# A spectral filter and MLP on one core: mirrored rows folded ahead of the transform along h, and that transform moved between the two mixings

## The chip, the cores and the metric

The kernel runs on one core of a Trainium2 chip. The metric is the device time of one execution in microseconds (us). The engines named here are TensorE (PE in the profile), VectorE (DVE), ScalarE (ACT), GpSimd (POOL) and SyncE (SP, which only issues DMAs).

## The reference

Two layers run over two images of 128 x 128 positions with 128 channels, in fp32. `afno_filter` mixes channels in the frequency domain, in blocks of 16 channels:

```python
def afno_filter(x, w1, b1, w2, b2):
    xf = jnp.fft.rfft2(x, axes=(1, 2), norm='ortho')
    ...
    o1r = jax.nn.relu(xr @ w1[0] - xi @ w1[1] + b1[0])   # einsum per block of channels
    o1i = jax.nn.relu(xi @ w1[0] + xr @ w1[1] + b1[1])
    o2r = o1r @ w2[0] - o1i @ w2[1] + b2[0]
    o2i = o1i @ w2[0] + o1r @ w2[1] + b2[1]
    ...                                                  # softshrink, 0.01
    return jnp.fft.irfft2(yf, s=(H, W), axes=(1, 2), norm='ortho') + x
...
    h = afno_filter(layer_norm(x, n1_g, n1_b), w1, b1, w2, b2) + x
    residual = h
    h = jax.nn.gelu(layer_norm(h, n2_g, n2_b) @ mw1 + mb1, approximate=False)
    return h @ mw2 + mb2 + residual
```

## The kernel before

The program makes four steps, one for each layer and image (`s` = 0 to 3). Each step has four stages on TensorE, one behind the other:

- `dft_w`: the transform along w, 128 matmuls of 128 x 128 x 128 (line 581), four into one PSUM bank. In step 0 ScalarE copies each bank to the arena in SBUF; in steps 1 to 3 ScalarE and VectorE take turns (line 362).
- `filter_`: 34 units, in 17 pairs (q = 0 and 1, one for each half of the channels). A unit goes through six operations on three engines: the transform along h (`dft_h`, line 591, four matmuls into bank q), a copy to `gsb` by ScalarE (`g_copy`, line 871), the first mixing (`mix1`, line 611, 64 x 64 tiles, bank 2 + q), bias and relu to `osb` by ScalarE (`o_relu`, line 878), the second mixing (`mix2`, line 649, 64 x 64 tiles, banks 4 to 7), and bias and softshrink by VectorE (`shrink`, lines 1119, 1121, 1134). Pair 1 has a single frequency only, and pairs 0 and 1 together need `edges` (line 688).
- `idft_h` (line 724), the inverse transform along h, whose banks ScalarE and VectorE copy out (line 389).
- `mlp`: the inverse transform along w (lines 743 and 749), layer norm, and the two products of the MLP with the gelu between them.

Nothing schedules this at run time: each engine runs its own instructions in the order of the program text, and counters (semaphores) hold one engine until another has come far enough. In the filter the order on TensorE is, for each p, mix1 of pair p + 1, mix2 of pair p, dft_h of pair p + 3. On ScalarE it is the two copies of pair p + 2, then the two relus of pair p + 1 (`batch`, line 959 and on).

What holds whom around the change:

- `gsb` and `osb` each have one buffer for each q. So `g_copy` of unit n waits until the first mixing of unit n - 2 has read `gsb` (`act.wait_ge(m1_mm, UNITS * s + n - 1)`), and `o_relu` of unit n until the second mixing of unit n - 2 has read `osb` (`act.wait_ge(m2_mm, UNITS * s + n - 1)`).
- `dft_h` of a unit writes bank q, and waits until the copy of the unit before it with the same q is done (`pe.wait_ge(g_out, ...)`).
- `mix1` of pair p + 1 waits for its two copies and for the relus of pair p, which read banks 2 and 3.
- `mix2` waits for its relu and for VectorE's first operation on the bank that it writes (`v_out`).

Of the kernel before, what the change touches and what calls it, by code (L numbers as in the profile page):

```python
# [75 lines left out]
CONSTS = 7 * P + MASKS  # L76
EVEN = KWS + 1
PB = 8
# [14 lines left out]
HELD_BANK = (6, 7, 0, 2)  # L93
# [9 lines left out]
def dft_constants():  # L103
# [10 lines left out]
    fh = np.concatenate([np.cos(turn * np.outer(h, k)), np.sin(turn * np.outer(h, k[1:-1]))], 1) * scale  # L114
    k_of = np.concatenate([k, -k[1:-1]])
    ih = np.concatenate([np.cos(turn * np.outer(k_of, h[:HALF + 1])),
                         np.sin(turn * np.outer(k_of, -h[HALF + 1:]))], 1) * scale

# [7 lines left out]
    parts = [fw.reshape(P, P), fh, ih, de.reshape(P, P).T, do.reshape(P, P).T, np.eye(P), reverse]  # L126
# [27 lines left out]
def afno(nc, x, consts, params, out):  # L154
    ctx = ExitStack()
    with ctx:
# [27 lines left out]
        paired = [a.rearrange("p (t h e) -> p t h e", h=H, e=2) for a in flat]  # L184
        spectra = [a.rearrange("p (k a g b d) -> p k a g b d", a=2, g=2, b=2, d=QUART) for a in flat]
        columns_of = [a.rearrange("p (q c k) -> p q c k", q=2, c=HALF) for a in flat]

        def rows_of(s):

            return paired[s % 2]  # L190

        def spec_of(s):

            return spectra[(s + 1) % 2]

# [14 lines left out]
        mask = cst[:, 7 * P:].rearrange("p (s b) -> p s b", s=4)  # L210
# [328 lines left out]
        def _(pe):  # L539
# [45 lines left out]
            def dft_h(s, n):  # L585
# [10 lines left out]
            def mix1(s, p):  # L596
# [39 lines left out]
            def mix2(s, p):  # L636
                kws = 1 if p == 1 else GROUP
                if s == 0 and p == 1:
                    pe.wait_ge(r_dve, R_DVE)
                if p >= 2:  # L640
                    pe.wait_ge(v_out, UNITS * s + 2 * p - 2)
                for q in range(2):
                    pe.wait_ge(o_out, UNITS * s + 2 * p + q + 1)
                    for i in range(kws):
                        at_ = GROUP * HALF * q + HALF * i
# [931 lines left out]
```

## Time and profile before

| | us |
|---|---|
| median of 3 runs | 1629.3 (1629.04 to 1630.48) |
| the profiled execution, its own time | 1629.48 |
| its span in the trace | 1627.7 |
| TensorE busy | 1556.1 (96%) |
| VectorE busy | 990.3 (61%) |
| ScalarE busy | 889.3 (55%) |
| GpSimd busy | 620.4 (38%) |

The span is the part of the execution that the trace covers; 1.8 us lie around it. An engine that is busy for most of the span is likely what bounds the kernel, but what one stage costs is read from the timeline of that stage: which engine works without a gap there, and what ends the gaps of the others.

### The profile page before, as it was taken

The page shows a single profiled execution, that of the slowest core. Times are in us where ns is not written, and L with a number is a line of the kernel's source. Part 1 is how long each engine was busy: PE and PEld are TensorE (multiplying, and loading weights), DVE is VectorE, ACT ScalarE, POOL GpSimd, SP SyncE. Part 2 cuts the span into 40 slices and gives each one's busy share as a digit, 9 for nine tenths or more (in the row PEclk, how much of TensorE's full clock was granted, in tenths as well). Part 3 has the DMA queues.
Part 4 walks back from the last instruction along what each step waited for, and adds up shares of the span by engine and source line. Part 5 has one row for each costly group of instructions (what it writes and reads, how often), then busy time and mean ns, then how long its engine had stood idle before and what let it go on. Part 6 is the DMA issues. An engine that isn't in the chain of part 4 may idle for free.

```text
span 1627.7 us, 43919 instructions
## 1 busy us (share of the span) xinstructions
PE 1556.1 (96%) x16132; PEld 1379.1 (85%) x16132; DVE 990.3 (61%) x2433; ACT 889.3 (55%) x1638; POOL 620.4 (38%) x782
## 2 busy tenths in 40 slices
PE   0999999999999899999999989999999989999999
PEld 0987888888998788888898888888889879888888
DVE  7967556656537665665655766565663675555553
ACT  5544366666534356666643436666662443666665
POOL 5800046776800017677660003667673000111111
PEclk9999999999999999999999999999999999999999
DMA  8410713333300062333420052333331006011111
GB/s 225 172 45 3 241 49 107 104 99 119 98 15 3 9 240 86 108 101 99 124 79 2 3 203 66 104 110 97 104 111 46 3 3 207 27 39 32 32 39 46
DMA packets 168583, 138.30 MB, mean 85 GB/s; under 512 B 10882, under 2 KB 132484, under 8 KB 168452
## 3 DMA queue, kind: packets, MB, share of 16 engines
q1 hardware_dynamic: 167268, 136.24, 26.6%
q8 instruction: 96, 1.57, 0.4%
q10 hardware_dynamic: 1184, 0.20, 0.1%
q14 instruction: 35, 0.29, 0.1%
HBM read 69.30 MB, written 67.11 MB: 84 GB/s over the span
## 4 chain that ended last, share of the span: by engine, by line
PE 93%; DVE 3%; ACT 1%; SPq 1%; DMA 1%; issue 1%; POOL 0%; ACTq 0%; DVEq 0%
PE ps L797 27%; PE ps L591 8%; PE ps L611 8%; PE ps L581 7%; PE ps L763 7%; PE ps L765 7%; PE ps L724 7%; PE ps L764 7%; PE ps L757 3%; PE ps L649 3%; PE ps L743 3%; PE ps L749 3%; SPq L431 1%; DMA first<-in_x_dram 1%; PE ps L779 1%
## 5 line engine op out<-in xcount | busy, mean ns | idle before, releaser
L797 PEld LDWEIGHTS ps<-mw,gel 128*128 128x128 f32 x4000 | 520.6, 191 | 42.3
L797 PE MATMUL ps<-mw,gel 128*128 128x128 f32 x4000 | 523.7, 274 | 0.0
L907 ACT ACTIVATE gel<-ps,mb1f 128x512 f32<-128x512 f32 x500 | 343.7, 687 | 250.6 <-PE ps L765 219.7
L1473 POOL TENSOR_TENSOR arena<-arena,mb2rep 128x512 f32<-128x512 f32 x125 | 160.2, 1282 | 634.5 <-ACT hn L893 634.5
L763 PE MATMUL ps<-hth,mw1h 128*128 128x512 f32 x512 | 259.7, 507 | 4.5 <-DVE vsb L1119 1.7
L1462 POOL TENSOR_SCALAR arena<-xnext,rstd,shift 128x128 f32<-128x128 f32 x360 | 159.4, 462 | 207.6 <-DVE shift L1356 207.6
L893 ACT ACTIVATE hn<-arena,shift,rstd 128x128 f32 (+1 forms) x512 | 221.6, 483 | 16.8 <-DVE shift L1356 16.8
L765 PE MATMUL ps<-hth,mw1l 128*128 128x512 f32 x512 | 202.1, 395 | 0.0
L764 PE MATMUL ps<-htl,mw1h 128*128 128x512 f32 x512 | 200.8, 392 | 0.0
L1203 DVE TENSOR_TENSOR arena<-ps,arena 128x512 f32 (+1 forms) x60 | 41.5, 691 | 252.0 <-PE ps L749 233.4
L871 ACT COPY gsb<-ps 128x512 f32<-128x512 f32 x128 | 69.1, 589 | 159.1 <-PE ps L611 153.0
L1220 DVE TENSOR_TENSOR htl<-ps,hth 128x512 fp32r<-128x512 f32 x128 | 88.2, 689 | 97.5 <-ACT hth L901 97.5
L1119 DVE TENSOR_TENSOR vsb<-ps,b2cols 128x512 f32<-128x512 f32 (+1 forms) x136 | 90.3, 664 | 88.2 <-PE ps L649 88.2
L611 PE MATMUL ps<-gsb,w1s 64*64 64x252 f32 (+5 forms) x2304 | 128.0, 359 | 9.2 <-ACT osb L878 6.2
L591 PE MATMUL ps<-cst,arena 128*128 128x128 f32 x1024 | 131.3, 281 | 2.3 <-ACT gsb L871 2.0
L1420 POOL TENSOR_TENSOR gz<-arena,gain 128x512 f32<-128x512 f32 x96 | 123.8, 1290 | 7.0
L591 PEld LDWEIGHTS ps<-cst,arena 128*128 128x128 f32 x1024 | 119.8, 191 | 6.9 <-ACT gsb L871 2.5
L581 PE MATMUL ps<-cst,arena 128*128 128x128 f32 x1024 | 121.4, 282 | 0.9 <-POOL arena L1433 0.9
L581 PEld LDWEIGHTS ps<-cst,arena 128*128 128x128 f32 x1024 | 120.9, 196 | 1.0 <-DVE arena L1085 1.0
L724 PEld LDWEIGHTS ps<-cst,arena 128*128 128x128 f32 x1024 | 115.3, 192 | 7.2 <-DVE arena L1134 6.2
L724 PE MATMUL ps<-cst,arena 128*128 128x128 f32 x1024 | 116.0, 275 | 4.7 <-DVE arena L1134 4.7
L901 ACT CAST hth<-ps 128x512 fp32r<-128x512 f32 x128 | 75.2, 587 | 80.1 <-PE ps L757 80.1
(111 smaller groups left out, 2125.6 us busy)
## 6 DMA issues: line engine op xcount, KB each, us to landing
arena<-aside SPq DMA_DIRECT2D x128, 256.0 KB, 4.8
aside<-gz SPq DMA_DIRECT2D x96, 256.0 KB, 3.0
between<-xout SPq DMA_DIRECT2D x62, 256.0 KB, 2.3
out_dram<-xout SPq DMA_DIRECT2D x62, 256.0 KB, 2.3
xnext<-between SPq DMA_DIRECT2D x60, 256.0 KB, 3.0
aside<-first SPq DMA_DIRECT2D x32, 256.0 KB, 2.3
xnext<-in_x_dram SPq DMA_DIRECT2D x30, 256.0 KB, 3.1
first<-in_x_dram SPq DMA_DIRECT2D x1, 960.0 KB, 7.4
```

Of the source, the lines that this page charges most:

```text
L581: mm = pe.matmul(ps[:, 2 + cg % 4, P * i:P * i + P], rows_of(s)[:, (GROUP * cg + i) // 2, :, i % 2], FW, start=True, stop=True)
L591: mm = pe.matmul(ps[:, q, P * i:P * i + P], spec_of(s)[:, GROUP * b + i, q].rearrange("p g r c -> p (g r c)"), FH, start=True, stop=True)
L611: mm = pe.matmul(to[:, :, dst[0]:dst[1]], w1s[own_rows, kind, q].rearrange("p r c -> p (r c)"), gsb[own_rows, q, j0:j1, src[0]:src[1]], st ...
L724: mm = pe.matmul(ps[:, cg % 4, P * i:P * i + P], y_of(s)[:, q, ch, :], IH, start=True, stop=True)
L763: pe.matmul(bank, h, hth[:, r % 2, :], start=True, stop=False)
L764: pe.matmul(bank, h, htl[:, r % 2, :], start=False, stop=False)
L765: pe.matmul(bank, l, hth[:, r % 2, :], start=False, stop=True).then_inc(f1_mm, 1)
L797: mm = pe.matmul(ps[:, r % 2, P * i:P * i + P], gel[:, r % 2, m, P * i:P * i + P], mw2[:, s // IMAGES, m, :], start=(m == 0 and i == 0), s ...
L893: ins = act.activation(hn[:, r % 2, i, :], row, ACT.Identity, bias=shift[:, r // 2, r % 2 * ROWS + i:r % 2 * ROWS + i + 1], scale=rstd[:, ...
L907: act.activation(gel[:, r % 2, m, :], ps[:, 2 + m % 2], ACT.Gelu, bias=mb1f[:, s // IMAGES, m:m + 1]).then_inc(gelu_out, 1)
L1462: ins = pool.tensor_scalar(zrow(s + 1, h0 + k), pairs(xnext[:, r, k, :]), rstd[:, r // 2, row:row + 1], shift[:, r // 2, row:row + 1], ALU ...
L1473: pool.tensor_tensor(t, t, b, ALU.add).then_inc(mb2_done, 1)
```

## The change

It has four parts. Those on steps 1 to 3 leave step 0 as it was.

1. **Folding (steps 1 to 3).** The rows of an image are laid in SBUF so that slot i and slot i + 64 hold rows that mirror each other. The transform along w is made in tiles of 128 rows by 64 columns: two channel groups, g = 0 and 1, go to the two halves of the PSUM partitions, the upper 64 slots to one bank and the lower 64 to the next (`mirrored`). ScalarE copies the upper bank to `hn`; VectorE writes the sum and the difference of both to the arena (`fold_out`, two operations for two banks).
2. **Transform along h in 64 x 64 tiles (steps 1 to 3).** The sums give the cosine part (65 columns), the differences the sine part (95 columns with the mirrored half). Both units of a pair go in one call, so that the four tiles of the array (two halves of the rows, two of the columns) are addressed one after another. The call waits for both copies. Step 0 keeps the 128 x 128 form, one unit behind the other.
3. **PSUM banks by unit.** The second mixing of q = 0 writes banks 4 and 5, that of q = 1 banks 6 and 7, each with a wait and a count of its own; before, a pair wrote 4 and 5 or 6 and 7 by turns and counted once. Two banks of the MLP's held tile move from 6 and 7 to 2 and 3.
4. **Order.** The transform along h of pair p + 3 is issued ahead of the second mixing of pair p, not behind it, in all four steps.

The inverse transform's columns, the rows that the last transform reads, and the VectorE operations behind it are turned round to the new order of rows; their number and size stay.

```diff
-HELD_BANK = (6, 7, 0, 2)
+HELD_BANK = (2, 3, 0, 2)
...
+        folded = [a.rearrange("p (k o a b d) -> p k o a b d", o=2, a=2, b=2, d=QUART) for a in flat]
...
             def evicted(s, cg):
                 if s == 0:
                     pe.wait_ge(a_act, cg + 1)
-                elif cg % 2:
-                    pe.wait_ge(a_dve, CGROUPS // 2 * (s - 1) + cg // 2 + 1)
-                else:
-                    pe.wait_ge(a_act, CGROUPS + CGROUPS // 2 * (s - 1) + cg // 2 + 1)
+                else:
+                    pe.wait_ge(a_dve, CGROUPS * (s - 1) + cg + 1)
...
                 for cg in range(CGROUPS):
-                    if s and cg == 3:
-                        pe.wait_ge(lo_out, TILES * s)
+                    if s:
+                        mirrored(s, cg // 2, cg % 2)
+                        continue
...
+            def mirrored(s, d, sign):
+
+                if d == 1 and sign:
+                    pe.wait_ge(lo_out, TILES * s)
+                if d >= 2 and not sign:
+                    evicted(s, 2 * d - 3)
+                q, slots = d // 8, slice(HALF, H) if sign else slice(0, HALF)
+                for i in range(GROUP):
+                    for g in range(2):
+                        t = KWS // 2 * q + KWS // 4 * g + GROUP // 2 * (d % 8) + i // 2
+                        mm = pe.matmul(ps[HALF * g:HALF * g + HALF, 2 + 2 * (d % 2) + sign, P * i:P * i + P],
+                                       rows_of(s)[:, t, slots, i % 2], FW, start=(i == 0), stop=True,
+                                       skip_group_check=True)
+                mm.then_inc(s1_mm, 1)
+
+            def dft_h(s, n, units=(0,)):
+                if s:
+                    g = spectrum_of(n + units[-1])
+                    if g >= 2:
+                        pe.wait_ge(g_out, 2 * BATCHES * s + g - 1)
+                    for i in range(GROUP):
+                        for o in range(2):
+                            for u in units:
+                                q = (n + u) % 2
+                                for x in range(2):
+                                    own_rows = slice(HALF * x, HALF * x + HALF)
+                                    cols = slice(HALF * (x ^ q), HALF * (x ^ q) + HALF)
+                                    dst = slice(P * i, P * i + EVEN) if o == 0 else slice(P * (i + 1) - FOLD_O, P * (i + 1))
+                                    mm = pe.matmul(ps[cols, q, dst],
+                                                   folded_of(s)[own_rows, GROUP * (g // 2) + i, o, q].rearrange(
+                                                       "p r c -> p (r c)"),
+                                                   FOLDS[o][own_rows], start=(i == 0 and o == 0), stop=True,
+                                                   skip_group_check=True)
+                    mm.then_inc(s2_mm, len(units))
+                    return
+                for u in units:
+                    whole_dft_h(s, n + u)
...
             def mix2(s, p):
                 kws = 1 if p == 1 else GROUP
-                if s == 0 and p == 1:
-                    pe.wait_ge(r_dve, R_DVE)
-                if p >= 2:
-                    pe.wait_ge(v_out, UNITS * s + 2 * p - 2)
                 for q in range(2):
+                    if p:
+                        pe.wait_ge(v_out, UNITS * s + 2 * p + q - 1)
+                    elif s == 0 and q:
+                        pe.wait_ge(r_dve, R_DVE)
+                    if p == EDGE_PAIR and q:
+                        pe.wait_ge(y_done, (UNITS + 1) * s + 2 * EDGE_PAIR + 1)
                     pe.wait_ge(o_out, UNITS * s + 2 * p + q + 1)
...
-                mm.then_inc(m2_mm, 2)
+                    mm.then_inc(m2_mm, 1)
...
                 for p in range(PAIRED):
                     if p + 1 < PAIRED:
                         mix1(s, p + 1)
-                    if p == EDGE_PAIR + 1:
-                        pe.wait_ge(y_done, (UNITS + 1) * s + 2 * EDGE_PAIR + 2)
-                    mix2(s, p)
+                    if p + 3 < PAIRED:
+                        dft_h(s, 2 * p + 6, (0, 1))
                     if p == EDGE_PAIR:
                         edges(s)
-                    if p + 3 < PAIRED:
-                        for q in range(2):
-                            dft_h(s, 2 * p + 6 + q)
+                    mix2(s, p)
...
                     if cg >= 4:
                         turned(s, cg - 4)
+                    elif s and cg >= 2:
+                        pe.wait_ge(gelu_out, CHUNKS * (TILES * s - 1) + cg - 1)
...
+            def upper_copy(s, q, j, r):
+
+                act.wait_ge(s1_mm, CGROUPS * s + CGROUPS // 2 * q + 4 * j + 2 * r + 1)
+                act.copy(hn[:, r].rearrange("p a b -> p (a b)"), ps[:, 2 + 2 * r]).then_inc(a_act, 1)
...
+            def fold_out(s, q, j, r):
+
+                dve.wait_ge(a_act, CGROUPS + CGROUPS // 2 * (s - 1) + CGROUPS // 4 * q + 2 * j + r + 1)
+                dve.wait_ge(s1_mm, CGROUPS * s + CGROUPS // 2 * q + 4 * j + 2 * r + 2)
+                upper = hn[:, r].rearrange("p a b -> p (a b)").rearrange("p (i k r) -> p k r i", i=GROUP, r=2)
+                lower_ = ps[:, 3 + 2 * r].rearrange("p (i k r) -> p k r i", i=GROUP, r=2)
+                for o, op in enumerate((ALU.add, ALU.subtract)):
+                    dst = folded_of(s)[:, :, o, q, :, bass.ds(GROUP * (2 * j + r), GROUP)]
+                    dve.tensor_tensor(dst, upper, lower_, op).then_inc(a_dve, 1)
...
-                at_ = GROUP * HALF * q
-                src = ps[:, 4 + 2 * odd:6 + 2 * odd, at_:at_ + HALF * kws].rearrange(
+                src = ps[:, 4 + 2 * q:6 + 2 * q, 0:HALF * kws].rearrange(
```

TensorE, step 0, in the middle of the filter. `gsb,w1s` is the first mixing, `w2s,osb` the second, `cst,arena` the transform along h. Before:

```order
22 L649 MATMUL ps<-w2s,osb 64x64 x32
23 L591 MATMUL ps<-cst,arena_51 128x128 x8
24 L611 MATMUL ps<-gsb,w1s 64x4x65 x4
25 L611 MATMUL ps<-gsb,w1s 64x4x63 x12
26 L649 MATMUL ps<-w2s,osb 64x64 x32
27 L591 MATMUL ps<-cst,arena_51 128x128 x8
28 L611 MATMUL ps<-gsb,w1s 64x4x65 x4
29 L611 MATMUL ps<-gsb,w1s 64x4x63 x12
30 L649 MATMUL ps<-w2s,osb 64x64 x32
```

The change at the same place:

```order
22 L649 MATMUL ps<-cst,arena_51 128x128 x8
23 L709 MATMUL ps<-w2s,osb 64x64 x32
24 L669 MATMUL ps<-gsb,w1s 64x4x65 x4
25 L669 MATMUL ps<-gsb,w1s 64x4x63 x12
26 L649 MATMUL ps<-cst,arena_51 128x128 x8
27 L709 MATMUL ps<-w2s,osb 64x64 x32
28 L669 MATMUL ps<-gsb,w1s 64x4x65 x4
29 L669 MATMUL ps<-gsb,w1s 64x4x63 x12
30 L649 MATMUL ps<-cst,arena_51 128x128 x8
```

The transform (x8, both units of a pair) stood behind the second mixing (x32), and stands ahead of it. (The lines are those of each program: `dft_h` is line 591 before and 649 behind the change, `mix1` 611 and 669, `mix2` 649 and 709.)

TensorE, step 1, a turn of the filter, before:

```order
334 L611 MATMUL ps<-gsb,w1s 64x4x65 x4
335 L611 MATMUL ps<-gsb,w1s 64x4x63 x12
336 L649 MATMUL ps<-w2s,osb 64x64 x32
337 L591 MATMUL ps<-cst,arena_50 128x128 x8
338 L611 MATMUL ps<-gsb,w1s 64x4x65 x4
339 L611 MATMUL ps<-gsb,w1s 64x4x63 x12
340 L649 MATMUL ps<-w2s,osb 64x64 x32
```

The change at the same place, one pair:

```order
366 L669 MATMUL ps<-gsb,w1s 64x4x65 x4
367 L669 MATMUL ps<-gsb,w1s 64x4x63 x12
368 L633 MATMUL ps<-cst,arena_50 64x65 x4
369 L633 MATMUL ps<-cst,arena_50 64x95 x4
370 L633 MATMUL ps<-cst,arena_50 64x65 x4
371 L633 MATMUL ps<-cst,arena_50 64x95 x4
372 L633 MATMUL ps<-cst,arena_50 64x65 x4
373 L633 MATMUL ps<-cst,arena_50 64x95 x4
374 L633 MATMUL ps<-cst,arena_50 64x65 x4
375 L633 MATMUL ps<-cst,arena_50 64x95 x4
376 L709 MATMUL ps<-w2s,osb 64x64 x32
377 L669 MATMUL ps<-gsb,w1s 64x4x65 x4
```

Eight matmuls of 128 x 128, which stood behind the second mixing, have become 32 of 64 x 64 with 65 and 95 columns, and stand between the two mixings.

VectorE, step 1, the first banks of the transform along w, before (with the semaphores waited for):

```order
537 L362 ISA [waits s1_mm]
538 L362 COPY arena_50<-ps 128x64x2x4
539 L1091 REGISTER_ALU
540 L362 ISA [waits s1_mm]
541 L362 COPY arena_50<-ps 128x64x2x4
```

The change:

```order
537 L1162 ISA [waits a_act]
538 L1167 ISA [waits s1_mm]
539 L1167 TENSOR_TENSOR arena_50<-hn,ps 128x64x2x4
540 L1167 ISA
541 L1167 TENSOR_TENSOR arena_50<-hn,ps 128x64x2x4
```

A copy of every second bank has become a sum and a difference for every two banks, which wait for ScalarE (`a_act`) and TensorE (`s1_mm`).

## Rows read from the trace of the kernel before

**Rows 1.** The page: engines' busy us; the chain that ended last, by engine

```profile
PE 1556.1 (96%) x16132; PEld 1379.1 (85%) x16132; DVE 990.3 (61%) x2433; ACT 889.3 (55%) x1638; POOL 620.4 (38%) x782
...
PE 93%; DVE 3%; ACT 1%; SPq 1%; DMA 1%; issue 1%; POOL 0%; ACTq 0%; DVEq 0%
```

**Rows 2.** Filter, steps 0, 3: length, busy PE, PEld, DVE, ACT, POOL, clock

```profile
76.53:163.55 87.02, 81.80 (x1898) 70.49 (x1896) 63.66 (x116) 37.39 (x67) 1.16 (x1) 1.00 0.11 37
...
1255.49:1342.54 87.05, 81.40 (x1889) 69.67 (x1887) 58.73 (x108) 38.19 (x68) 0.00 (x0) 1.00 0.01 3
```

**Rows 3.** Timeline, PE, step 1's filter: start, duration, line, out<-in, count

```profile
505.88 1.94 PE L611 MATMUL ps<-gsb,w1s 64*64 64x260 f32 x32
507.64 1.11 PE L649 MATMUL ps<-w2s,osb 64*64 64x64 f32 x64
508.68 2.05 PE L591 MATMUL ps<-cst,arena 128*128 128x128 f32 x16
510.66 1.94 PE L611 MATMUL ps<-gsb,w1s 64*64 64x260 f32 x32
512.42 1.11 PE L649 MATMUL ps<-w2s,osb 64*64 64x64 f32 x64
```

**Rows 4.** Timeline of ScalarE and VectorE in the same turn

```profile
507.88 1.07 ACT L871 COPY gsb<-ps 128x512 f32<-128x512 f32 x2 [2.52 <-PE ps L611]
...
508.82 0.69 DVE L1119 TENSOR_TENSOR vsb<-ps,b2cols 128x512 f32<-128x512 f32 x1 [0.89 <-PE ps L649]
508.88 1.27 ACT L878 ACTIVATE osb<-ps,vectors 128x512 f32<-128x512 f32 x2
```

**Rows 5.** Timeline of step 1's filter, behind the short second mixing

```profile
483.00 0.41 PE L649 MATMUL ps<-w2s,osb 64*64 64x64 f32 x16
483.25 1.07 ACT L871 COPY gsb<-ps 128x512 f32<-128x512 f32 x2 [3.17 <-PE ps L611]
...
483.88 2.05 PE L591 MATMUL ps<-cst,arena 128*128 128x128 f32 x16 [0.47 <-ACT gsb L871]
```

**Rows 6.** Timeline of the last two pairs of step 1's filter

```profile
550.32 1.14 PE L649 MATMUL ps<-w2s,osb 64*64 64x64 f32 x64
551.53 0.69 DVE L1119 TENSOR_TENSOR vsb<-ps,b2cols 128x512 f32<-128x512 f32 x1 [0.53 <-PE ps L649]
551.59 1.27 ACT L878 ACTIVATE osb<-ps,vectors 128x512 f32<-128x512 f32 x2 [3.15 <-PE ps L649]
...
552.42 1.18 PE L649 MATMUL ps<-w2s,osb 64*64 64x64 f32 x64 [0.96 <-ACT osb L878]
```

**Rows 7.** The transform along w, step 1: stretch, then VectorE's copies

```profile
439.82:469.97 30.15, 30.15 (x258) 30.15 (x257) 11.06 (x16) 9.38 (x16) 9.07 (x8) 1.00 0.16 53
...
L362 DVE COPY arena<-ps x48: 691/692/693, 442.0 to 1255.8; 128x512 f32 x48
...
466.53 0.69 DVE L362 COPY arena<-ps 128x512 f32 x1 [1.19 <-PE ps L581]
```

**Rows 8.** Timeline of VectorE ahead of it: a sum of PSUM and SBUF

```profile
435.06 0.69 DVE L1234 TENSOR_TENSOR xout<-ps,arena 128x512 f32<-128x512 f32 x1
435.67 2.15 DVE L1365 TENSOR_SCALAR arena<-xlast,rstd,shift 128x128 f32<-128x128 f32 x8
```

**Rows 9.** Timeline of the start of step 1's filter

```profile
469.97 2.30 PE L591 MATMUL ps<-cst,arena 128*128 128x128 f32 x16
...
472.31 0.59 ACT L871 COPY gsb<-ps 128x512 f32<-128x512 f32 x1 [0.58 <-PE ps L591]
...
473.04 2.14 PE L611 MATMUL ps<-gsb,w1s 64*64 64x195 f32 x64 [0.77 <-ACT gsb L871]
```

**Rows 10.** Two stretches at the end of step 1's filter

```profile
545.00:549.00 4.00, 2.46 (x96) 2.01 (x92) 2.78 (x5) 2.26 (x4) 0.00 (x0) 1.00 0.00 0
553.00:557.00 4.00, 2.23 (x47) 1.51 (x38) 3.86 (x8) 1.38 (x2) 0.00 (x0) 1.00 0.01 4
```

**Rows 11.** Timeline of VectorE in step 2: weights scaled between copies

```profile
849.78 0.72 DVE L1022 TENSOR_SCALAR w1s<-w1s,swapped 128x64 f32<-128x64 f32 x4
```

More of the change, by code:

```diff
@@ L75 @@
 MASKS = 4 * BLOCKS
-CONSTS = 7 * P + MASKS
 EVEN = KWS + 1
+FOLD_E, FOLD_O = EVEN, P - EVEN + KWS // 2
+MASK_AT = 7 * P + FOLD_E + FOLD_O
+CONSTS = MASK_AT + MASKS
 PB = 8
@@ L113, in dft_constants @@
     fw[:, 0, 1] = cos[:, KWS]
-    fh = np.concatenate([np.cos(turn * np.outer(h, k)), np.sin(turn * np.outer(h, k[1:-1]))], 1) * scale
-    k_of = np.concatenate([k, -k[1:-1]])
+    ks = np.concatenate([[0, KWS], np.arange(2, KWS, 2), np.arange(1, KWS, 2)])
+    fh = np.concatenate([np.cos(turn * np.outer(h, ks)), np.sin(turn * np.outer(h, ks[2:]))], 1) * scale
+    k_of = np.concatenate([ks, -ks[2:]])
+    fold_e, fold_o = fh[:HALF, :EVEN].copy(), fh[:HALF, P - FOLD_O:].copy()
+    fold_e[-1] = scale * (ks % 2 == 0)
+    fold_o[:, :KWS // 2] = 0
+    fold_o[-1] = -scale * (np.arange(FOLD_O) < KWS // 2)
+    folds = np.tile(np.concatenate([fold_e, fold_o], 1), (2, 1))
     ih = np.concatenate([np.cos(turn * np.outer(k_of, h[:HALF + 1])),
                          np.sin(turn * np.outer(k_of, -h[HALF + 1:]))], 1) * scale
+    ih[:, HALF:] = ih[:, :HALF - 1:-1].copy()
     de = 2 * np.stack([cos, -sin], 2)[:, :KWS]
@@ L209, in afno @@
         FW, FH, IH, DE, DO, IDENT, REVERSE = (cst[:, i * P:(i + 1) * P] for i in range(7))
-        mask = cst[:, 7 * P:].rearrange("p (s b) -> p s b", s=4)
+        FOLDS = tuple(cst[:, 7 * P + a:7 * P + b] for a, b in ((0, FOLD_E), (FOLD_E, FOLD_E + FOLD_O)))
+        mask = cst[:, MASK_AT:].rearrange("p (s b) -> p s b", s=4)
         w1s = sb("w1s", [P, 4, 2, 2, QUART])
@@ L648, in mix2 @@
                                 own_rows, k = slice(HALF * g, HALF * (g + 1)), slice(HALF * c, HALF * (c + 1))
-                                mm = pe.matmul(ps[k, 4 + 2 * (p % 2) + g, at_:at_ + HALF], osb[own_rows, q, i, k],
+                                mm = pe.matmul(ps[k, 4 + 2 * q + g, at_:at_ + HALF], osb[own_rows, q, i, k],
                                                w2s[own_rows, q].rearrange("p r c -> p (r c)"), start=True, stop=True)
-                mm.then_inc(m2_mm, 2)
+                    mm.then_inc(m2_mm, 1)
             def filter_(s):
@@ L709, in first_pair @@
                 t = slice(GROUP // 2 * a, GROUP // 2 * b)
-                for bank, m, h0 in ((6, DE, 0), (7, DO, H - ROWS)):
+                for bank, m, h0 in ((6, DE, 0), (7, DO, HALF)):
                     dst = ps[:, bank - (2 if a else 0), 0:ROWS * GROUP * (b - a)]
@@ L745, in idft_w @@
                     dst = ps[:, 7].rearrange("p (t h e) -> p t h e", h=ROWS, e=2)
-                    pe.matmul(dst[:, :, 1:], DO, odd[:, :, 1:], start=True, stop=True, skip_group_check=True)
-                    mm = pe.matmul(dst[:, :, 0], DE, odd[:, :, 0], start=False, stop=True, skip_group_check=True)
+                    pe.matmul(dst[:, :, :3], DO, odd[:, :, :3], start=True, stop=True, skip_group_check=True)
+                    mm = pe.matmul(dst[:, :, 3], DE, odd[:, :, 3], start=False, stop=True, skip_group_check=True)
                 else:
@@ L931, in _ @@
                     act.wait_ge(mb2_done, TILES * s)
-                for q in range(2):
-                    for g in range(2):
-                        with act.Fori(0, CGROUPS // 16) as j:
-                            for r in ((0, 2) if s else range(4)):
-                                a_out(s, q, g, j, r)
+                if s == 0:
+                    for q in range(2):
+                        for g in range(2):
+                            with act.Fori(0, CGROUPS // 16) as j:
+                                for r in range(4):
+                                    a_out(s, q, g, j, r)
+                else:
+                    for q in range(2):
+                        with act.Fori(0, CGROUPS // 8) as j:
+                            for r in range(2):
+                                upper_copy(s, q, j, r)
                 if s:
@@ L1263, in _ @@
                     for q in range(2):
-                        for g in range(2):
-                            with dve.Fori(0, CGROUPS // 16) as j:
-                                for r in (1, 3):
-                                    a_out(s, q, g, j, r)
+                        with dve.Fori(0, CGROUPS // 8) as j:
+                            for r in range(2):
+                                fold_out(s, q, j, r)
                         if q == 0 and s % IMAGES == 0:
@@ L1457, in z_rows @@
                 def z_rows(j, r):
-                    h0 = ROWS * tile_of(j, r)
+                    h0 = zplace(j, r)
                     for k in range(ROWS):
                         row = (2 + r % 2) * ROWS + k
-                        ins = pool.tensor_scalar(zrow(s + 1, h0 + k), pairs(xnext[:, r, k, :]), rstd[:, r // 2, row:row + 1],
+                        ins = pool.tensor_scalar(zrow(s + 1, h0 + (ROWS - 1 - k if r % 2 else k)), pairs(xnext[:, r, k, :]), rstd[:, r // 2, row:row + 1],
                                                  shift[:, r // 2, row:row + 1], ALU.mult, ALU.add)
```

67 lines of the change are left out of this document (34 added, 33 removed).

## Prediction

> **What bounds the kernel now.** I read the page first: TensorE is busy for 1556.1 of 1627.7 us, and 93% of the chain that ended last lies on it [rows 1]. So a saving on TensorE counts, and so does every gap that opens there. The four filters take 87.0 to 87.1 us each, at a granted clock of 1.00 [rows 2]. Then I read one turn of the filter in the timeline: the first mixing starts at 505.88, the second at 507.64, the transform along h at 508.68, the next first mixing at 510.66. TensorE does not wait, and from one second mixing to the next it takes 4.78 us: 1.77 for mix1, 1.04 for mix2, 1.98 for the transform [rows 3]. The other two engines do wait in that turn, and what for decides this case. ScalarE's two copies start 0.24 us behind the end of mix1, last 1.07 us, and had waited 2.52 us for it; its two relus follow at 508.88; VectorE starts 0.14 us behind the end of mix2 [rows 4]. So a turn is a ring: mix1, copies, relus, next mix1. Today mix2 and the transform, 3.02 us together, lie between the first mixings and hide both copies and relus.
>
> **Order: the first wait.** The copies into `gsb` wait for mix1 of pair p + 1, which reads the one buffer of each q. The transform of pair p + 3 waits for those copies, since it writes the banks that they read. It now stands right behind that mix1. What this costs is seen where little work lies between: behind the short second mixing of pair 1, mix1 ends at 483.00, the copies start at 483.25 and the transform at 483.88, with TensorE idle for 0.47 us [rows 5]. So from the end of mix1, a transform that needs the first copy alone starts 0.88 us later, and one that needs both (end at 483.25 + 1.07, and 0.04) 1.36 us later. Step 0 pays 0.88, steps 1 to 3 pay 1.36. Behind TensorE's waiting instruction stand mix2 of pair p, whose data lie ready, and the next mix1.
>
> **Order: the second wait.** The relus of pair p + 1 wait until mix2 of pair p has read `osb`, and the next mix1 waits for them. Before, the transform stood between; now mix1 follows mix2 at once. The price is in the last pairs, where no transform is left: mix2 starts at 550.32 and lasts 1.04, so it ends at 551.36; both relus start at 551.59 (0.23 behind) and last 1.27 together, and TensorE stands idle for them [rows 6]. In the change each unit of mix2 counts by itself, so the first relu starts 0.52 us earlier: 0.23 - 0.52 + 1.27 + 0.04 = 1.02 us from the end of mix2 to the next mix1. Bounds: 0.96 (the wait in the last row, for one relu behind a full mix2) and 1.54 (0.23 + 1.27 + 0.04, if the split count brings nothing). I take 1.02, which follows from the code's own counts.
>
> **The transform along h in small tiles.** No row shows 64 x 64 tiles with 65 and 95 columns, but two rows lie around them. mix1 is 32 instructions, 8 rounds over the four tiles with 254 columns on average, in 1.77 us: 221 ns a round. mix2 is 64 instructions, 16 rounds with 64 columns, in 1.04 us: 65 ns a round [rows 3]. The line through both is 12.5 ns and 0.82 ns a column. A pair's transform is 16 rounds with 80 columns on average: 16 x (12.5 + 65.7) = 1.25 us. Low end 1.05 (columns alone), high end 1.98 (the price of today's form). I take 1.25, as both neighbours have its tiles: 0.73 us less than before on each of 14 pairs.
> The Trainium skill, "TensorEngine Tiling (Array Packing)", section Restrictions and Gotchas, says that different row tiles cannot access the same PSUM bank at once, and both row tiles of a unit write bank q here. By that the tiles would go two at a time and the turn would be some 1.25 us longer. The row speaks against it: `mix1` also writes bank 2 + q from both halves of the rows, and 8 rounds of four take 1.77 us, not twice that.
>
> **The turn.** Steps 1 to 3: 1.77 + 1.36 + 1.25 + 1.04 + 1.02 = 6.44 us against 4.78, 1.66 more. Step 0: 1.77 + 0.88 + 1.98 + 1.04 + 1.02 = 6.69, 1.91 more. There are 14 such turns in a filter (p = 0 to 13), and 0.5 us of waiting at pair 1 is there already [rows 5]. Step 0: 14 x 1.91 - 0.5 = 26.2 us. Each other step: 14 x 1.66 - 0.5 = 22.7 us, 68.2 for three. The tail (pairs 14 to 16) has no transform and stays.
>
> **The transform along w.** 256 matmuls with two instructions each make 256 rounds over two tiles of 128 columns: 256 x (12.5 + 105) = 30.1 us, against 30.15 now [rows 7]. Low end 27 (columns alone). I take no change. Its eviction goes to VectorE: for two banks, a sum and a difference of one operand in PSUM and one in SBUF. The nearest such row takes 0.69 us, and the next operation starts 0.61 behind it [rows 8], so a fold ends 0.14 + 0.61 + 0.69 = 1.44 us behind the lower bank, where TensorE takes 30.15 / 16 = 1.88 for the two banks in between. VectorE had 1.19 us to spare ahead of each copy [rows 7]. So TensorE hides the fold, with 0.4 us to spare; if an operation took 1.0 us instead, a fold would cost 0.3 us each, 14 us in three steps.
> The Trainium skill, "TensorE: Matmul & The Clock Gate", section Part 3 on packing small matmuls, says that a weight load overlaps a running matmul only where the row groups differ. The two new tiles share all rows, so by it they would go one after the other. In [rows 7] 257 weight loads, all in the same row group, lie beside as many matmuls in 30.15 us, so here they do overlap.
>
> **Small terms.** At the start of the filter the second unit's transform waits for the last fold: 1.48 us behind the end of the transform along w, then 1.25, then the copy and its latencies as now (0.87), 3.6 us against 473.04 - 469.97 = 3.07 [rows 9]: 0.5 x 3 = 1.5 us. In step 2 VectorE scales the weights in mid-transform, 1.6 us for ten small operations of which the last four are in [rows 11]; 0.4 us of slack a fold and a bank in reserve leave 0.7 us of it exposed. The waits of the inverse transform for the held tile's gelu, the reversed rows and the moved banks cost nothing: those gelus are done before the inverse transform starts (TensorE still waits for VectorE's last softshrink then), and instruction numbers and sizes are the same.
>
> **Sum.** 26.2 + 68.2 + 1.5 + 0.7 = 96.6 us. The profiled execution took 1629.48 us (1627.7 of span and 1.8 around it), 0.2 over the median of 1629.3. So 1629.5 + 96.6 = 1726.
>
> **Rivals.**
> *Only the first wait binds.* If the relus did not hold the next mix1, a turn would be 5.42 us (5.67 in step 0): (14 x 0.64 - 0.5) x 3 + 14 x 0.89 - 0.5 + 2.2 = 39 us, 1669. Against it: the relus' wait of 3.15 us for mix2 [rows 6] is in the code as well.
> *Faster.* If TensorE found all its inputs ready, a turn would be 1.77 + 1.25 + 1.04 = 4.06 us, 0.73 less in 42 turns: -31 + 2, 1601. It holds if copies and relus run beside mix1 and mix2, for which `gsb` and `osb` would need a second buffer each. It decides where less than 0.73 of the 2.38 us of waiting remains. ScalarE's own work, 2.34 us a turn, and VectorE's, 3.8, would allow it; the wait of 2.52 us for mix1 [rows 4] speaks against it.
> *Small tiles two at a time in the transform along h.* 32 rounds, 2.50 us, 1.25 more in 42 turns: +53, 1779.
> *Column tiles one at a time in the transform along w.* 512 rounds, 60 us: +30 in each of three steps, 1816. Against it: mix2's four tiles, two of which share rows, need 65 ns a round of 53 ns of columns.
> *The clock falls.* TensorE would be busy for 4.06 of 6.44 us, 63%. In two stretches of 4 us with it busy for 2.46 and 2.23 us the granted clock was 1.00 [rows 10]. At half of it (1.2 instead of 2.4 GHz) each turn would grow by some 4 us: 14 x (3 x 4.06 + 4.79) = 238, some 1960.
>
> **How the numbers follow.** Forecast 82%, only the first wait 5%, two at a time 4%, column tiles 3%, clock 2%, faster 3%, and 1% that gains and waits cancel. Low end: both transforms at column price, -0.2 x 42 - 3 x 3 = -17, 1709. High end: today's price of the transform along h, +0.73 x 42 = +31, and 3 for folds, 1760. Chances: faster by over 0.2% 3%, within 0.2% (about what a measurement of this kernel can tell from no change) 1%, slower 96%.
>
> **What would show it.** In steps 1 to 3, about 6.4 us from one second mixing to the next; TensorE idle for about 1.1 to 1.3 us ahead of the transform, released by ScalarE's `gsb` copy, and about 1.0 us ahead of the first mixing, released by `osb`; a filter of about 110 us in steps 1 to 3 and 113 in step 0; a transform along w of about 30 us; VectorE's folds at 0.69 us. The forecast is wrong if either idle time is missing, if a pair's transform takes 2 us or more, or if the transform along w is far from 30.

## The result, and the profile after

The change took 1742.5 us (median of 4 runs, 1741.6 to 1743.5), the kernel before 1629.2 beside it: 1.069 times as long (95% interval 1.068 to 1.071), 113 us more. The forecast was 1726, the range 1709 to 1760.

The page of the changed kernel, engines' busy us and the chain that ended last, answers to [rows 1]:

```profile
PE 1542.3 (89%) x19204; PEld 1347.2 (77%) x19204; DVE 1055.6 (61%) x2481; ACT 894.5 (51%) x1638; POOL 618.7 (36%) x782
...
PE 83%; ACT 6%; issue 5%; DVE 4%; SPq 1%; DMA 1%; ACTq 0%; DVEq 0%; POOL 0%
```

TensorE is busy for 14 us less than before and its share falls from 96% to 89%. In the chain, ScalarE has gone from 1% to 6% and "issue" from 1% to 5%. Two groups of the page, with the idle time ahead of them, tell where (columns: busy us, mean ns of one, idle us before and its releaser):

```profile
L669 PE MATMUL ps<-gsb,w1s 64*64 64x252 f32 (+5 forms) x2304 | 128.6, 359 | 66.2 <-ACT osb L941 63.0
...
L633 PE MATMUL ps<-cst,arena 64*64 64x65 f32 (+1 forms) x3072 | 69.3, 232 | 53.2 <-ACT gsb L934 49.9
```

The first mixing has 66.2 us of idle time ahead of it, released by the relus of line 941; the transform along h in small tiles has 53.2, released by the copies to `gsb` (line 934). One turn of step 1's filter, all engines (columns as in [rows 3] and [rows 4]):

```profile
527.49 1.95 PE L669 MATMUL ps<-gsb,w1s 64*64 64x260 f32 x32 [1.07 <-ACT osb L941]
...
529.50 1.07 ACT L934 COPY gsb<-ps 128x512 f32<-128x512 f32 x2 [2.15 <-PE ps L669]
...
530.62 1.35 PE L633 MATMUL ps<-cst,arena 64*64 64x65 f32 x64 [1.18 <-ACT gsb L934]
...
531.79 1.11 PE L709 MATMUL ps<-w2s,osb 64*64 64x64 f32 x64
532.51 0.69 DVE L1193 TENSOR_TENSOR vsb<-ps,b2cols 128x512 f32<-128x512 f32 x1 [2.82 <-PE ps L709]
532.57 1.26 ACT L941 ACTIVATE osb<-ps,vectors 128x512 f32<-128x512 f32 x2 [2.00 <-PE ps L709]
...
533.98 1.32 PE L669 MATMUL ps<-gsb,w1s 64*64 64x260 f32 x20 [1.07 <-ACT osb L941]
```

This is the ring of the prediction: mix1 at 527.49, copies at 529.50, transform at 530.62 behind 1.18 us of idleness, mix2 at 531.79, relus at 532.57 (the first half of mix2 is done then), next mix1 at 533.98 behind 1.07 us. A turn takes 6.49 us, against 4.78 in [rows 3]. In step 0, where the transform has its old form:

```profile
98.13 2.05 PE L649 MATMUL ps<-cst,arena 128*128 128x128 f32 x16 [0.75 <-ACT gsb L934]
100.11 1.16 PE L709 MATMUL ps<-w2s,osb 64*64 64x64 f32 x64
102.28 1.95 PE L669 MATMUL ps<-gsb,w1s 64*64 64x260 f32 x32 [1.01 <-ACT osb L941]
104.99 2.05 PE L649 MATMUL ps<-cst,arena 128*128 128x128 f32 x16 [0.75 <-ACT gsb L934]
```

Here a turn takes 6.86 us. Where the 112.1 us that the span has gained lie, read from the first matmul of each stage (us):

| step | transform along w, before | after | filter, before | after | rest, before | after |
|---|---|---|---|---|---|---|
| 0 | 30.2 | 30.2 | 87.0 | 115.0 | 276.3 | 276.4 |
| 1 | 30.2 | 33.8 | 87.1 | 111.3 | 275.8 | 275.8 |
| 2 | 30.3 | 35.7 | 87.1 | 110.8 | 275.2 | 275.3 |
| 3 | 30.2 | 33.8 | 87.1 | 110.5 | 285.2 | 285.1 |

The filters have gained 99.4 us, the transforms along w 12.7, the rest nothing. The stretches of step 1's two stages and of step 0's filter (columns as in [rows 2]):

```profile
467.61:501.44 33.83, 31.25 (x513) 27.73 (x513) 31.41 (x31) 9.37 (x16) 8.96 (x8) 1.00 0.14 48
501.44:612.76 111.32, 74.27 (x2657) 61.15 (x2655) 60.32 (x110) 39.59 (x68) 0.00 (x0) 1.00 0.01 3
76.24:191.25 115.01, 86.30 (x1898) 72.08 (x1896) 63.82 (x116) 38.84 (x67) 1.11 (x1) 1.00 0.08 28
```

VectorE is busy for 31.41 of 33.83 us in the transform along w, where it was for 11.06 of 30.15 in [rows 7]. Its folds, by line, and TensorE in that stage:

```profile
L1167 DVE TENSOR_TENSOR arena<-hn,ps x96: 1016/1073/1118, 469.7 to 1345.4; 128x512 f32 x96
```

```profile
467.61 3.72 PE L615 MATMUL ps<-cst,arena 128*64 128x128 f32 x64
471.88 3.99 PE L615 MATMUL ps<-cst,arena 128*64 128x128 f32 x64 [0.55 <-DVE arena L1167]
476.13 4.01 PE L615 MATMUL ps<-cst,arena 128*64 128x128 f32 x64 [0.27 <-DVE arena L1167]
```

A fold operation takes 1073 ns, not 0.69 us as in [rows 8], and TensorE now waits for VectorE in this stage.

### The profile page after: what moved, and what is told of

It reads as the page before. It is cut to its first block, busy times and chain, and to the rows that moved or that the text cites. A ratio compares the mean times of both kernels' runs of the same rounds, so it can differ in the third digit from the quotient of the medians.

```text
span 1739.8 us, 50215 instructions
## 1 busy us (share of the span) xinstructions
PE 1542.3 (89%) x19204; PEld 1347.2 (77%) x19204; DVE 1055.6 (61%) x2481; ACT 894.5 (51%) x1638; POOL 618.7 (36%) x782
## 4 chain that ended last, share of the span: by engine, by line
PE 83%; ACT 6%; issue 5%; DVE 4%; SPq 1%; DMA 1%; ACTq 0%; DVEq 0%; POOL 0%
PE ps L855 26%; PE ps L669 7%; PE ps L821 7%; PE ps L823 7%; PE ps L782 7%; PE ps L822 7%; PE ps L633 4%; PE ps L615 3%; PE ps L815 3%; PE ps L801 3%; ACT osb L941 3%; PE ps L807 3%; ACT gsb L934 2%; PE ps L709 2%; PE ps L649 2%
## 5 line engine op out<-in xcount | busy, mean ns | idle before, releaser
L669 PE MATMUL ps<-gsb,w1s 64*64 64x252 f32 (+5 forms) x2304 | 128.6, 359 | 66.2 <-ACT osb L941 63.0
L941 ACT ACTIVATE osb<-ps,vectors 128x512 f32<-128x512 f32 (+1 forms) x136 | 84.4, 666 | 141.1 <-PE ps L709 128.7
L669 PEld LDWEIGHTS ps<-gsb,w1s 64*64 64x64 f32 (+1 forms) x2304 | 88.9, 132 | 87.5 <-issue 74.3
L782 PEld LDWEIGHTS ps<-cst,arena 128*128 128x128 f32 x1024 | 115.3, 192 | 4.9 <-DVE arena L1208 3.9
L782 PE MATMUL ps<-cst,arena 128*128 128x128 f32 x1024 | 116.1, 275 | 2.4 <-DVE arena L1208 2.4
L633 PE MATMUL ps<-cst,arena 64*64 64x65 f32 (+1 forms) x3072 | 69.3, 232 | 53.2 <-ACT gsb L934 49.9
L633 PEld LDWEIGHTS ps<-cst,arena 64*64 64x64 f32 x3072 | 59.8, 133 | 72.2 <-ACT gsb L934 67.8
```

The costliest lines, as they stand in the source:

```text
L633: mm = pe.matmul(ps[cols, q, dst], folded_of(s)[own_rows, GROUP * (g // 2) + i, o, q].rearrange("p r c -> p (r c)"), FOLDS[o][own_rows], s ...
L669: mm = pe.matmul(to[:, :, dst[0]:dst[1]], w1s[own_rows, kind, q].rearrange("p r c -> p (r c)"), gsb[own_rows, q, j0:j1, src[0]:src[1]], st ...
L782: mm = pe.matmul(ps[:, cg % 4, P * i:P * i + P], y_of(s)[:, q, ch, :], IH, start=True, stop=True)
L941: act.activation(dst, ps[:, 2 + q, 0:P * kws], ACT.Relu, bias=b1v[:, q:q + 1]).then_inc(o_out, 1)
```

## The experiments

Theory: most of the added time is a ring of four links (mix1, `gsb` copies, the transform and mix2, relus), whose two waits of about 1.2 and 1.1 us were hidden before by what stood between; the rest is the fold's slow read. Rivals: the small tiles or the folds carry the loss; only one of the waits counts; the order costs by itself.

**The order alone undone.**

```diff
                         mix1(s, p + 1)
-                    if p + 3 < PAIRED:
-                        dft_h(s, 2 * p + 6, (0, 1))
                     if p == EDGE_PAIR:
                         edges(s)
                     mix2(s, p)
+                    if p + 3 < PAIRED:
+                        dft_h(s, 2 * p + 6, (0, 1))
```

> The change with its order alone undone: in all four steps the transform along h of pair p + 3 stands behind the second mixing of pair p again; folds, small tiles and banks by unit stay. Ring theory (the added time is the two waits in a turn, for the gsb copies and for the relus): a turn falls from 6.49 to about 4.35 us in steps 1 to 3 (1.77 for mix1, then 1.38 until both copies are done, which hides the second mixing, then 1.18 for the transform) and from 6.86 to 4.79 in step 0. 14 x 2.14 x 3 + 14 x 2.07 = 119 us less than the change's 1742.5: 1624. Rival (the folds and the small tiles carry the added time, the order little): 1700 or more.

Measured: 1641.2 us (1637.3 to 1643.3), 1.007 times the kernel before (1.005 to 1.008). So the order carries 101 of the 113 us. The rows of TensorE in step 1's filter:

```profile
491.26 1.95 PE L669 MATMUL ps<-gsb,w1s 64*64 64x260 f32 x32
493.01 1.14 PE L709 MATMUL ps<-w2s,osb 64*64 64x64 f32 x64
494.40 1.35 PE L633 MATMUL ps<-cst,arena 64*64 64x65 f32 x64 [0.25 <-ACT gsb L934]
495.66 1.95 PE L669 MATMUL ps<-gsb,w1s 64*64 64x260 f32 x32
...
511.71 1.07 PE L709 MATMUL ps<-w2s,osb 64*64 64x64 f32 x55
513.24 0.35 PE L709 MATMUL ps<-w2s,osb 64*64 64x64 f32 x9 [0.46 <-issue]
```

The regular turn is 4.40 us (491.26 to 495.66), as the theory had it, with 0.25 us of waiting left ahead of the transform. But 17 us are missing against the 1624 expected. In the last row TensorE stops for 0.46 us in the midst of a second mixing, and "issue" means that it waits for nothing that the profile shows. Such pauses are in no filter of before or of the change; here there are 15 of them in the filters of steps 1 to 3, 7.9 us together. At most 3.4 us more are two spells of half clock (see the last section). Another part lies in the first turns of a filter, which had less to gain than the 2.14 us that the expectation gave each of 14: the second turn of step 1's filter takes 4.86 us in the change and 4.11 here.

**The order alone, on the kernel before.**

```diff
                     if p == EDGE_PAIR + 1:
                         pe.wait_ge(y_done, (UNITS + 1) * s + 2 * EDGE_PAIR + 2)
+                    if p + 3 < PAIRED:
+                        for q in range(2):
+                            dft_h(s, 2 * p + 6 + q)
                     mix2(s, p)
                     if p == EDGE_PAIR:
                         edges(s)
-                    if p + 3 < PAIRED:
-                        for q in range(2):
-                            dft_h(s, 2 * p + 6 + q)
```

> The kernel before with the order alone changed: the transform along h of pair p + 3 ahead of the second mixing of pair p; no folds, no small tiles, and both units of a second mixing counted at its end. Ring theory: the two waits come here too, and the second is 1.5 us, since the first relu waits for the whole second mixing: a turn of 7.3 us in all four steps, 56 x 2.45 = 137 us over the kernel before: 1760 to 1768. If banks and counts by unit shorten nothing, a turn is 6.86 as in step 0 of the change: 1629 + 56 x 2.07 = 1745. Rival (the order is harmless without folds and small tiles): 1629.

Measured: 1762.3 us (one run), 133 more than before. A regular turn:

```profile
553.28 1.95 PE L611 MATMUL ps<-gsb,w1s 64*64 64x260 f32 x32 [1.54 <-ACT osb L878]
555.92 2.05 PE L591 MATMUL ps<-cst,arena 128*128 128x128 f32 x16 [0.69 <-ACT gsb L871]
557.90 1.16 PE L649 MATMUL ps<-w2s,osb 64*64 64x64 f32 x64
560.60 1.94 PE L611 MATMUL ps<-gsb,w1s 64*64 64x260 f32 x32 [1.54 <-ACT osb L878]
```

The profile shows 1.54 us of idle time ahead of mix1. On the prediction's own measure, from the start of mix2 plus 1.04 us, it is 1.66 (558.94 to 560.60), 0.12 over the bound of 1.54 that it gave for two relus behind a whole mix2. A turn takes 7.32 us, as expected. Against this, step 0 of the change (6.86 us, with the same transform) gets 0.5 us back from the banks and counts by unit: the order with its penalty is worse without them.

**A second `osb` buffer.** A relu then waits for the second mixing of two pairs before.

```diff
-        osb = at("osb", [P, 2, GROUP, P], o); o += size(osb.shape)
+        osb = at("osb", [P, 2, 2, GROUP, P], o); o += size(osb.shape)
...
-                if not (isinstance(n, int) and n < 2):
-                    act.wait_ge(m2_mm, UNITS * s + n - 1)
-                dst = osb[:, q, 0:kws, :].rearrange("p j k -> p (j k)")
+                if n >= 4:
+                    act.wait_ge(m2_mm, UNITS * s + n - 3)
+                dst = osb[:, n // 2 % 2, q, 0:kws, :].rearrange("p j k -> p (j k)")
```

> The change with a second osb buffer for each unit, so that a relu waits for the second mixing of two pairs before; ScalarE's loop over pairs is written out. Ring theory: the wait of 1.07 us ahead of the first mixing goes, the one ahead of the transform stays; a turn is 5.42 us in steps 1 to 3 and 5.8 in step 0, 56 x 1.07 = 60 us less: 1683. Rival (the first mixing waits for something else that is late as well, or the saved wait moves ahead of the transform): within 15 us of 1742.

Measured: 1685.1 us (one run), 57 less than the change, where 60 were expected. ScalarE's loop over pairs is also written out here, which was not tried by itself.

```profile
525.77 1.90 PE L669 MATMUL ps<-gsb,w1s 64*64 64x260 f32 x32
528.92 1.35 PE L633 MATMUL ps<-cst,arena 64*64 64x65 f32 x64 [1.25 <-ACT gsb L934]
530.09 1.11 PE L709 MATMUL ps<-w2s,osb 64*64 64x64 f32 x64
531.02 1.91 PE L669 MATMUL ps<-gsb,w1s 64*64 64x260 f32 x32
```

The first mixing follows the second without a wait, and the 1.25 us ahead of the transform stay: a turn of 5.25 us. So the two waits are two, each with its own buffer behind it.

**The fold's operand laid out by ScalarE.**

```diff
-                act.copy(hn[:, r].rearrange("p a b -> p (a b)"), ps[:, 2 + 2 * r]).then_inc(a_act, 1)
+                laid = hn[:, r].rearrange("p a b -> p (a b)").rearrange("p (k r i) -> p k r i", i=GROUP, r=2)
+                act.copy(laid, ps[:, 2 + 2 * r].rearrange("p (i k r) -> p k r i", i=GROUP, r=2)).then_inc(a_act, 1)
...
-                upper = hn[:, r].rearrange("p a b -> p (a b)").rearrange("p (i k r) -> p k r i", i=GROUP, r=2)
+                upper = hn[:, r].rearrange("p a b -> p (a b)").rearrange("p (k r i) -> p k r i", i=GROUP, r=2)
```

> The change with one edit: ScalarE writes the upper bank to hn in the order in which VectorE's fold reads it, so that the fold's operand in SBUF is contiguous; its PSUM operand and its destination keep their patterns. Theory (a fold takes 1.07 us, not 0.69, because it reads hn in single elements 512 bytes apart): folds fall to 0.69 us, the transform along w from 33.8 to 30.1 us and the start of the filter from 4.5 to 3.6, some 4.6 us in each of three steps: 1728 to 1730. Rival (two inputs with patterns of four levels, or the destination's pattern, make it slow): folds stay at 1.07 and the time at 1742.

Measured: 1722.3 us (two runs), 20 less than the change; 13 had been expected.

```profile
L1168 DVE TENSOR_TENSOR arena<-hn,ps x96: 680/682/690, 469.6 to 1326.1; 128x512 f32 x96
```

```profile
467.46 28.20 PE L615 MATMUL ps<-cst,arena 128*64 128x128 f32 x512
495.59 1.34 PE L633 MATMUL ps<-cst,arena 64*64 64x65 f32 x32
```

The fold falls from 1073 to 682 ns, with its PSUM operand and its destination untouched. The scattered read of `hn` was the cause. The transform along w falls to 28.1 us, 2 less than its old form: 512 instructions of 128 x 64 at 55 ns.

**The order undone and `hn` laid out.** The edits of the first and of the fourth experiment together, on the change.

> Both edits at once: the transform along h stands behind the second mixing again, and ScalarE lays hn out as the fold reads it. If the two costs are independent, the second edit brings what it brought to the change (33.8 to 28.1 us for the transform along w and 0.7 us at the start of the filter, 20 us in all) and the time is 1641 - 20 = 1621, some 8 us under the kernel before. Rival (without the fold's stalls TensorE only meets the same wait later in the filter): above 1632.

Measured: 1616.8 us (1615.3 to 1619.1), 0.992 times the kernel before (0.991 to 0.994). The second edit brings 24 us here, some 4 more than in the change; single filters differ by up to 3 us between the two profiled executions, through the pauses and through the two spells of half clock that the first of them had. This beats both kernels, by 12.7 and 126 us.

**A second `gsb` buffer on top.**

```diff
-EARLY = 13
+EARLY = 14
...
-        gsb = at("gsb", [P, 2, GROUP, P], o); o += size(gsb.shape)
+        gsb = at("gsb", [P, 2, 2, GROUP, P], o); o += size(gsb.shape)
...
-                    act.wait_ge(m1_mm, UNITS * s + n - 1)
-                act.copy(gsb[:, q].rearrange("p j k -> p (j k)"), ps[:, q]).then_inc(g_out, 1)
+                    act.wait_ge(m1_mm, UNITS * s + n - 3)
+                act.copy(gsb[:, spectrum_of(n) // 2 % 2, q].rearrange("p j k -> p (j k)"), ps[:, q]).then_inc(g_out, 1)
```

> As the kernel with both edits, and a second gsb buffer for each unit, so that the copies of a pair run while the first mixing reads the other buffer; EARLY goes from 13 to 14 to make room, and ScalarE's loop over pairs is written out. Ring theory: the last wait of a turn (0.25 us ahead of the transform) and the 0.14 behind it go, a turn is TensorE's own 1.77 + 1.18 + 1.04 = 3.99 us against 4.40: 42 x 0.41 = 17 us less, 1604. Rival (TensorE's instructions come too slowly: in the kernel with the order undone it pauses for 0.4 to 0.8 us in the midst of groups, waiting for nothing that the profile shows, while its instruction queue moves 16 KB every 3.7 us): a turn stays at 4.3 or more and the time at 1617 or more.

Measured: 1615.5 us (1615.5 to 1617.3), 0.992 times the kernel before (0.990 to 0.993), 1.3 us under the kernel without the buffer, where 13 had been expected. Most turns of step 1's filter take 4.1 to 4.5 us. So the rival holds in its mechanism, though its own figure was 1617 or more. TensorE in step 1's filter:

```profile
527.84 1.30 PE L633 MATMUL ps<-cst,arena 64*64 64x65 f32 x63
529.08 1.10 PE L669 MATMUL ps<-gsb,w1s 64*64 64x260 f32 x15
530.65 1.23 PE L669 MATMUL ps<-gsb,w1s 64*64 64x252 f32 x17 [0.48 <-issue]
531.56 1.14 PE L709 MATMUL ps<-w2s,osb 64*64 64x64 f32 x60
```

No wait for `gsb` is left, but pauses stand in the midst of groups (0.48 us inside this first mixing). Step 1's filter had 4.6 us of them, in 9 places, all four filters 17.1 us in 33. The queue that fetches instructions, in the same 40 us (505 to 545) of the kernel before and of this one:

```profile
q8 instruction: 7, 0.11, 1.2%
```

```profile
q8 instruction: 11, 0.18, 1.9%
```

It moves 7 packets of 16 KB before, one every 5.5 us, and 11 here, one every 3.65 us. That these are TensorE's instructions follows from the counts: the small tiles add 6144 loads and matmuls to the program (2 x 19204 against 2 x 16132), and the queue moves 120 packets instead of 96, so a packet holds 256 instructions.

The times of the single packets, which the trace holds, tie the pauses to them. In the filters of the six kernels that pause (the second `osb` buffer, the order undone alone, then with `hn` laid out, then with the second `gsb` buffer, and the two kernels below), TensorE stops 120 times without a wait that the profile shows. Each of the 120 pauses ends 1.2 to 1.6 us after a packet of this queue has ended. By chance few would: of all matmuls in step 1's filter of this kernel, 10% start in that stretch behind a packet. In no trace of this case do two packets start less than 3.3 us apart. From this an estimate: 320 instructions a turn take 320 / 256 packets, at least 4.1 us on average. The expectation of 1604 had TensorE's own work, 3.99 us, as the only limit.

**The change's own order, with both buffers doubled.** The edits of the two buffers and of `hn` together, on the change.

> The change in its own order, with hn laid out for the fold and second buffers for both gsb and osb (EARLY 14, ScalarE's loop written out). Ring theory: copies and relus no longer lie between two operations of TensorE, so the order costs nothing: a turn of about 4.0 us in steps 1 to 3 and 4.79 in step 0, within 5 us of the kernel with the order undone and a second gsb buffer: 1604 to 1610. Rival (the order itself costs, for example by what each engine finds ready): most of the 100 us that remain of the change's loss stay, 1700 or more.

Measured: 1619.8 us (0.994, 0.992 to 0.996). That is 10 us over the expected 1604 to 1610, which took over the 17 us missed above, but within 5 us of the kernel with the order undone and a second `gsb` buffer. The same order that cost 101 us costs 4 once both buffers are doubled. So nearly all of its price was that of the copies and relus which it uncovered. The 4 us left need not be the order's either: the filters of this trace have 19.5 us of pauses in 34 places, and the granted clock stood at half in four spells, against one in the trace that it is compared with.

**The same work for the queue, more for the array.** On the kernel with the second `gsb` buffer, the cosine matmuls are widened by zeros.

```diff
-FOLD_E, FOLD_O = EVEN, P - EVEN + KWS // 2
+FOLD_E, FOLD_O = P, P - EVEN + KWS // 2
...
+    fold_e = np.concatenate([fold_e, np.zeros((HALF, P - EVEN))], 1)
...
-                                    dst = slice(P * i, P * i + EVEN) if o == 0 else slice(P * (i + 1) - FOLD_O, P * (i + 1))
+                                    dst = slice(P * i, P * i + FOLD_E) if o == 0 else slice(P * (i + 1) - FOLD_O, P * (i + 1))
```

> The kernel with both edits and the second gsb buffer, and the cosine matmuls of the small transform widened from 65 to 128 columns by zeros in the table, so that they add nothing to the output. The number of instructions stays; TensorE's own work grows by 8 rounds x 63 columns x 0.82 ns = 0.41 us a turn, 42 turns, 17 us. Theory (in these kernels the instructions come too slowly: one packet of 16 KB, 256 instructions, every 3.6 us, however short the ring is): most of the added work fills the pauses, of which step 1's filter had 4.6 us in 9; 1616 rises by 0 to 8 us and the pauses shrink. Rival (the pauses are something of the array or of its tiles, not of the supply): the pauses stay and the time rises by 17 us, to 1632.

Measured: 1619.1 us (1617.7 to 1620.0), 3.6 more for 17 us of added work. The pauses of step 1's filter fell from 4.6 us in 9 places to 2.0 in 4, those of all four filters from 17.1 us in 33 to 8.8 in 18. So the pauses are filled by work that needs no further instructions. With the packets' times above, this puts the limit of these filters on the supply of instructions: the 18 pauses that are left also end 1.3 to 1.6 us behind a packet.

## Why the prediction was right, and where it was off

**The two waits.** Right. Ahead of the transform 1.38 us were measured between the end of mix1 and the transform (529.24 to 530.62; the end is 527.49 + 1.75, the time from mix1 to the next operation with the order undone, 491.26 to 493.01), 1.36 forecast; from the end of mix2 to mix1 1.15 (531.79 + 1.04 to 533.98), 1.02 forecast. The transform in small tiles takes 1.17 us (530.62 to 531.79), 1.25 forecast. A turn is 6.49 us against 6.44, so two small errors cancel in part. The one in the second wait can be named: I took 0.04 us from the end of the relus to the next operation, which is what lies between the first copy and the transform in [rows 5], but in [rows 6] a single relu ends at about 552.27 (it lasts 0.68 us) and the second mixing that needs it starts at 552.42, 0.15 later. In the change it is 0.15 too (533.83 to 533.98). In step 0 it is 6.86 against 6.69: the wait ahead of the transform is 0.94 us, not 0.88, and mix2 with the relus behind it takes 2.17, not 2.06. The four filters gained 99.4 us, where the terms for waits and filter start add up to 95.9.

**The transform along w.** Here the sum was short. The term was 0 us and 0.7 for step 2; measured were 12.7. TensorE's rate was not at fault (28.1 us once nothing held it, 30.1 forecast). The mis-sized term for 11 of these us is the fold: I priced it at 0.61 and 0.69 us by a sum whose SBUF operand is contiguous [rows 8], and it took 1.07. The prediction had this case as an aside (1.0 us, 14 us in all), but neither the sum nor the range carried it: the high end holds 3 us for folds. The time lies within the range because the 31 us that it allowed for the transform along h were not needed. The slow fold also moved the start of the filter, 4.5 us behind the end of the transform (501.44 to 505.94 in step 1) where 3.6 were forecast. The scaling of the weights in step 2 cost 1.9 us, not 0.7 (35.7 against 33.8 in the other steps); TensorE waits there for one fold behind it:

```profile
911.59 3.94 PE L615 MATMUL ps<-cst,arena 128*64 128x128 f32 x64 [2.01 <-DVE arena L1167]
```

The edit of `hn` gives 20 us back, more than the 16.5 that the forecast missed, because the unhindered transform is also quicker than the old one.

**The rivals.** That only the first wait binds is refuted by the second `osb` buffer, which took out 57 us. That small tiles go two at a time, or column tiles one at a time, is refuted by 1.17 us for a pair's transform and 28.1 us for the transform along w. The Trainium skill's rule on row tiles and PSUM banks ("TensorEngine Tiling (Array Packing)", Restrictions and Gotchas) therefore does not hold for this use: both row tiles of a unit write one bank, and 16 rounds of four tiles take 1.17 us. The faster case was put down to second buffers for `gsb` and `osb`. With both doubled (and `hn` laid out) the change's order did give a time under the kernel before, 1619.8, but not the 1601 worked out, since the supply of instructions took the place of the waits.

**The clock.** In the profiled execution of the changed kernel it stayed at 1.00; two of the four executions had a mean of 0.999 and took 1743.2 and 1743.5 us, the others 1741.6 and 1741.9. It fell for short whiles in the traces of five experiments; see below.

## What to carry to other kernels

When an operation is moved on the busiest engine, ask first what it stood between: here 3 us of TensorE work covered 1.1 us of copies and 1.3 us of relus on another engine, and with one buffer for each of them their whole latency came back in each turn. Before an order is judged by itself, look at which buffers make its waits; with two of each the order cost 4 us instead of 101. And price a new operand by its access pattern, not by its size.

## What the runs showed of the hardware

- VectorE, 128 x 512 fp32, one operand in PSUM and one in SBUF: 682 ns with the SBUF operand contiguous, 1073 ns with it read in single elements 512 bytes apart. Both kernels read PSUM in that scattered order, and a copy from PSUM in the same order took 692 ns [rows 7]. Of the fold's three accesses only the scattered read from SBUF was seen to cost time.
- Two column tiles of 128 x 64 share all rows and still overlap fully: 512 instructions in 28.1 us, 55 ns each with 128 columns, against 118 ns for each of 256 instructions of 128 x 128.
- TensorE's instructions come in packets of 16 KB, 256 instructions each, and no two packets started less than 3.3 us apart. Where a filter used one every 5.5 us no pause was seen; in the kernels that used one every 3.7 to 4.8 us TensorE paused for 0.2 to 1.7 us at a time without a wait, and went on 1.2 to 1.6 us after a packet had ended, each time. Splitting matmuls into small tiles raises this demand: 320 loads and matmuls a turn, against 224.
- The granted clock stood at half for 3.4 us at a time in the midst of five experiments' traces: the order undone (twice), the order alone on the kernel before (once), the second `osb` buffer (three times), the second `gsb` buffer (once) and both buffers (four times). Executions of the kernel before with a mean clock of 0.998 or 0.999 took 1630.2 to 1630.6 us, those with 1.000 took 1629.0 to 1629.5. One of the spells, with the order undone, in step 2 (columns as in [rows 2]):

```profile
850.00:855.00 5.00, 4.67 (x82) 4.20 (x80) 5.00 (x14) 1.27 (x3) 0.00 (x0) 1.00 0.00 0
855.00:857.00 2.00, 0.73 (x14) 0.49 (x10) 1.45 (x4) 0.48 (x1) 0.00 (x0) 1.00 0.03 8
857.00:860.00 3.00, 2.26 (x24) 2.26 (x26) 2.61 (x3) 0.49 (x1) 0.00 (x0) 0.67 0.01 3
860.00:863.00 3.00, 3.00 (x44) 2.88 (x40) 1.66 (x2) 0.68 (x2) 0.00 (x0) 0.76 0.00 0
```

TensorE had waited 2.01 us for a fold behind the scaling of the weights, and was busy for 0.73 of the 2 us of the second row; then the clock fell to half (1.2 instead of 2.4 GHz), from 858.05 to 861.46. The same wait stands in the trace of the change (at 911.59, above), and the clock did not fall there.
